# Attention and routed experts on one core: split parts stored once, tables stored in parts of five and three tiles, far rows on GpSimd's queue, shares spread by TensorE

## The chip, the core and the metric

The kernel runs on one core of a Trainium2 chip, in one launch. The metric is the device time of the program in microseconds (us), as a median over runs. The engines are TensorE (PE; its weight loads are PEld), VectorE (DVE), ScalarE (ACT), GpSimd (POOL) and SyncE (SP), which only issues transfers and waits. One core has 16 DMA engines.

## The reference, cut to what matters

`x` is 4 x 1024 tokens of 256 features, and every layernorm is over the features.

```python
h = layernorm(x)
q, k, v = h @ Wq + bq, h @ Wk + bk, h @ Wv + bv            # 16 heads of 16
pos_k = rel_embeddings @ Wk + bk                            # 128 relative positions
c2p = take_along_axis(q @ pos_k.T, clip(rel + 64, 0, 127))
p2c = swapaxes(take_along_axis(k @ pos_k.T, clip(-rel + 64, 0, 127)))
probs = softmax((q @ k.T + c2p + p2c) / sqrt(48))
out = (probs @ v) @ Wo + bo + h
x = x + layernorm(layernorm(out) * ln_scale + ln_bias)
y = layernorm(x)                                            # then 8 experts, top 1
e = argmax(softmax(y @ Wr + br))
# every expert sees y where it was chosen and zeros elsewhere; all eight results are added
x = x + layernorm(sum_i(relu((y * (e == i)) @ W1[i] + b1[i]) @ W2[i] + b2[i]))
```

`rel` is a log bucket of the distance: within 128 positions it varies, and beyond that it is constant on either side ("far").

## The kernel before, in words

The program has five stages, one after another, each a block that all engines enter and leave together.

`spread` (to 38 us) makes the position tables and stores them.

`project` (38 to 200 us) walks over 8 groups of 512 tokens. It normalises them, turns them with PE, makes q, k and v, and splits q and k into three bf16 parts (high, middle, low) so that bf16 products can stand for f32 ones. The parts are stored in `split_d` as six slots of each side, because an attention product uses six pairs of parts: one part goes to three slots, one to two, one to one. SP issues 12 stores of a group in L363. Small far products go to `far_d` (L369), normalised rows plus `bo` to `xn_d` (made by POOL in L551), and v to `v_d`.

`attend` (200 to 1490 us) walks over 64 units (4 batches x 16 heads), each of 8 tiles of 128 queries. Each unit first has its position products made by PE (`make_table`, two units ahead). ACT copies them out (L859), SP writes them to DRAM (`skew_write`, L655) and, when they have landed, reads them back skewed by one element for each row (`skew_read`, L665). POOL then mends the edges of the band in five steps (`edge`, L926 to L942). After the last step of a half it raises `near_made`, for which the PE products of that half of the tiles wait (`score`, L740). The order on SP for each pass `u` is written out by hand:

```python
skew_read(u + 1, 1); skew_write(u + 2, 0); load_unit(u + 4); store(u - 2)
skew_read(u + 2, 0); skew_write(u + 2, 1)
```

`load_unit` reads the six slots of q and of k of one unit, 96 rows of 2 KB on each side, in one transfer each (L637), and the far rows in three small ones (L642). It waits until the unit that used the buffers has been flipped: for unit u + 4 that is the last flip of unit u - 2, which PE makes in step 8u + 4, just ahead of the scores of tile 4 of unit u (`LAG` is 13 steps).

PE's order in step s is: flip half 0 of unit-tile s - 13, make table s + 16, flip half 1, score s, weigh s - 14, and in the second step of a unit `turn_top` (L785), which waits for five small POOL operations (`split_top`). POOL's order is also written out, by step s: the entries of `steps` say in which step which steps of `edge` of which half are made.

`mix` (1490 to 1690 us) walks over 16 groups of 256 tokens: heads and softmax shares are loaded, multiplied, projected by Wo, normalised three times and stored, with the routing behind it. In each of its first 8 steps 1 MB of W2 is loaded (L1119). `experts` (1690 to 2002 us) does the experts' products.

Of the kernel before, what the change touches and what calls it, by code (L numbers as in the profile page):

```python
# [35 lines left out]
QSLOTS = ((0, 1, 3), (3, 1, 2), (5, 1, 1))  # L36
KSLOTS = ((1, 2, 3), (2, 2, 2), (0, 1, 1))
# [16 lines left out]
def constants():  # L54
# [28 lines left out]
    steps[:, ET + 8 + P:] = np.arange(NT)[None, :] * P + np.arange(P)[:, None] + 1  # L83
    sel = np.zeros((P, E), np.float32)
    for j in range(4):
        sel[32 * j:32 * j + E] = 1.0 - np.eye(E)
    return dict(c_pick=pick, c_masks=masks, c_fold=fold, c_side=side, c_steps=steps, c_sel=sel)


def build(nc, x, Wq, bq, Wk, bk, Wv, bv, Wo, bo, rel_emb, ln_s, ln_b, W1, b1, W2, b2, Wr, br,  # L90
          c_pick, c_masks, c_fold, c_side, c_steps, c_sel, out):
    ctx = ExitStack()
    with ctx:
        sem = Rack(lambda name: ctx.enter_context(nc.semaphore(name)))

        def dram(name, shape, dt=F32):
# [3 lines left out]
        xn_d = dram("xn_d", [TOK, D])  # L100
        split_d = dram("split_d", [2, TERMS, N * DH, S], BF16)
        far_d = dram("far_d", [2, N, 2, PARTS, S], BF16)
# [8 lines left out]

        spread(nc, sem, Wk, bk, rel_emb, c_pick, c_masks, c_side, pick_d, posT_d)
        spent = sem.spend()
        project(nc, sem, spent, x, Wq, bq, Wk, bk, Wv, bv, bo, c_masks, posT_d, xn_d, split_d, far_d, v_d)
# [8 lines left out]
        mix(nc, sem, spent, x, xn_d, ctx_d, share_d, Wo, ln_s, ln_b, Wr, br, b1, W2, b2, c_masks, c_steps, c_sel, rows_d, bias_d,  # L123
            total_d, w2_all, idx_in, idx_out, expert)
# [44 lines left out]
def spread(nc, sem, Wk, bk, rel_emb, c_pick, c_masks, c_side, pick_d, posT_d):  # L169

    with ExitStack() as ctx:
# [26 lines left out]
        def _(sp):  # L198
# [9 lines left out]
            for tab in range(2):  # L208
                for n, (first, step, many) in enumerate((KSLOTS, QSLOTS)[tab]):
                    for slot in range(first, first + step * many, step):  # L210
# [57 lines left out]
def project(nc, sem, spent, x, Wq, bq, Wk, bk, Wv, bv, bo, c_masks, posT_d, xn_d, split_d, far_d, v_d):  # L268
# [5 lines left out]
    with ExitStack() as ctx:  # L274
# [8 lines left out]
        bv_b, bo_b = sb("bv_b", [P, D]), sb("bo_b", [P, D])  # L283
# [4 lines left out]
        xnb = [sb(f"xnb{i}", [P, GT, D]) for i in range(2)]  # L288
        v32 = [sb(f"v32_{i}", [P, GT, VROW]) for i in range(2)]
        stats, mv = sb("stats", [P, 2, GT, 6]), sb("mv", [P, 2, GT, 2])  # L290
        var, root, inv, shift = (sb(w, [P, 2, GT]) for w in ("var", "root", "inv", "shift"))
# [13 lines left out]
        xn_out, xnb_made = [sem(f"p_xn_out{i}") for i in range(2)], sem("p_xnb_made")  # L305
# [17 lines left out]
        def _(sp):  # L323
# [7 lines left out]
            for semaphore in spent:  # L331
# [7 lines left out]
                     (bv_b[:, :], view(bv.tensor, 0, [[0, P], [1, D]])),  # L339
                     (bo_b[:, :], view(bo.tensor, 0, [[0, P], [1, D]]))]  # L340
            assert len(loads) == 8
# [6 lines left out]
            for s in range(-2, NG + 1):  # L348
                g = s + 2
                if live(g):  # L350
                    sp.wait_ge(xnb_made, g + 1)
                    sp.dma_start(view(xn_d, g * G * D, [[D, P], [P * D, GT], [1, D]]), xnb[g % 2][:, :, :]
                                 ).then_inc(xn_out[g % 2], 16)
                    if live(g + XB):
                        load(g + XB)
                g = s - 1
                if live(g):
                    b, half = g // 2, g % 2
                    sp.wait_ge(lo_made, g + 1)
# [7 lines left out]
                    for m in range(4):  # L367
                        at = (m // 2 * N + b * H + m % 2 * 8) * 2 * PARTS * S + half * G
                        sp.dma_start(view(far_d, at, [[PARTS * S, 16], [S, PARTS], [1, G]]),  # L369
                                     far_part[g % 2][32 * m:32 * m + 16, :, :]).then_inc(far_out[g % 2], 16)  # L370
# [5 lines left out]
            for i in range(2):  # L376
                sp.wait_ge(v_out[i], 16 * (NG // 2))
                sp.wait_ge(split_out[i], 16 * 12 * (NG // 2))
                sp.wait_ge(far_out[i], 16 * 4 * (NG // 2))
                sp.wait_ge(xn_out[i], 16 * (NG // 2))  # L380

        @block.vector
        def _(dve):
# [3 lines left out]
            for s in range(-3, NG + 1):  # L387
                g = s + 2
                if live(g):
                    dve.wait_ge(root_made, g + 1)  # L390
                    nc.vector.reciprocal(inv[:, g % 2, :], root[:, g % 2, :]).then_inc(inv_made, 1)
                    dve.wait_ge(inv_made, g + 1)
                    nc.vector.scalar_tensor_tensor(shift[:, g % 2, :], mv[:, g % 2, :, 0], -1.0, inv[:, g % 2, :],
                                                   ALU.mult, ALU.mult).then_inc(shift_made, 1)
# [26 lines left out]
                if live(g):  # L421
                    if g == 0:
                        dve.wait_ge(loaded, 16 * 9)
# [15 lines left out]
        def _(act):  # L439
# [4 lines left out]
            def normal(g, t):  # L444
                if t == 0:
                    act.wait_ge(shift_made, g + 1)
                    if g >= NB:
                        act.wait_ge(x_turned, g - NB + 1)
                        act.wait_ge(xnb_made, g - NB + 1)
# [1190 lines left out]
```

## Time and profile before

| | |
|---|---|
| median of 3 runs | 2007.51 us (2007.21 to 2009.05) |
| profiled execution, its own time | 2003.63 us |
| span of the profile | 2001.7 us |
| busy in the span | PE 85%, DVE 68%, ACT 56%, POOL 53%, PEld 58% |
| moved by DMA | 453.36 MB, mean 226 GB/s |
| queue of SP | 415.25 MB, 65.2% of the 16 engines' time |
| SP's stores of parts | 32 of 384 KB, 32 of 256 KB, 32 of 128 KB |

A share of busy time is a mean over stages that have different limits. "DMA share" is the mean busy share of the 16 DMA engines: 0.5 can mean all of them half of the time, or eight of them all of the time. A wait of SP counts from its last instruction.

### The profile page before, as it was taken

How to read it: one execution, taken by the hardware profiler on the slowest of the kernel's cores; microseconds unless marked ns; L12 is line 12 of the kernel's file. 1: busy time of each engine (PE TensorE's matmuls, PEld its weight loads, DVE VectorE, ACT ScalarE, POOL GpSimd, SP SyncE). 2: the span in 40 equal slices, each digit the busy share in tenths (PEclk: the TensorE clock that was granted, in tenths of full speed). 3: DMA queues.
4: the chain of work that ended last, by engine and by line, in shares of the span. 5: the costliest groups of instructions: out<-in, count | busy, mean ns of one | idle time of the engine just before them, and what ended most of it. 6: DMA issues, size and time to landing. Idle time of an engine off the chain costs nothing. (4 is left out here: it accounts for less than half of the span.)

```text
span 2001.7 us, 40568 instructions
## 1 busy us (share of the span) xinstructions
PE 1698.0 (85%) x13688; PEld 1159.6 (58%) x13688; DVE 1370.7 (68%) x3938; ACT 1121.8 (56%) x2233; POOL 1069.1 (53%) x1268
## 2 busy tenths in 40 slices
PE   1882389999999999999999999999973674999997
PEld 1451156565656566566565666566532464999996
DVE  1673188788888788898798899899843553343343
ACT  1672257676767677677677777677751460222221
POOL 0210267676777667667576777777711451233332
PEclk6996589999999999999999999999996675999998
DMA  4598778777777777777877777787718852676772
GB/s 113 188 303 274 225 250 262 246 237 251 245 261 248 256 247 240 257 254 245 265 237 251 249 261 250 240 272 246 235 44 215 284 176 86 198 212 215 223 219 78
DMA packets 320826, 453.36 MB, mean 226 GB/s; under 512 B 35132, under 2 KB 260303, under 8 KB 320526
## 3 DMA queue, kind: packets, MB, share of 16 engines
q1 hardware_dynamic: 308034, 415.25, 65.2%
q10 hardware_dynamic: 7596, 21.10, 3.4%
q0 software_dynamic: 4992, 14.43, 1.9%
q8 instruction: 112, 1.84, 0.4%
q14 instruction: 92, 0.75, 0.1%
HBM read 257.32 MB, written 193.65 MB: 225 GB/s over the span
## 5 line engine op out<-in xcount | busy, mean ns | idle before, releaser
L865 ACT ACTIVATE t_probsT<-t_flip 128x512 f32<-128x512 f32 x1024 | 619.2, 607 | 242.7 <-PE t_flip L756 117.5
L814 DVE TENSOR_REDUCE t_most<-t_scores 128x1 f32<-128x640 f32 (+1 forms) x512 | 436.7, 853 | 169.8 <-PE t_scores L740 166.5
L833 DVE TENSOR_SCALAR t_band<-t_band,t_top 128x384 f32<-128x384 f32 (+1 forms) x512 | 383.8, 750 | 0.0
L859 ACT COPY t_table<-t_table_ps 128x512 f32<-128x512 f32 x512 | 298.2, 582 | 70.7 <-issue 41.1
L777 PE MATMUL t_sum_ps<-t_probsT,t_vals 128*32 128x256 f32 x4096 | 329.5, 394 | 0.2 <-ACT t_probsT L865 0.2
L926 POOL TENSOR_TENSOR t_near<-t_near,t_masks 128x384 f32<-128x384 f32 (+1 forms) x128 | 146.8, 1147 | 338.9 <-DMA t_near<-skew_d 336.4
L942 POOL TENSOR_TENSOR t_near<-t_near,t_masks 128x768 f32<-128x768 f32 (+1 forms) x128 | 272.4, 2129 | 0.0
L763 PE MATMUL t_flip<-t_masks,t_band 128*128 128x128 f32 x1408 | 263.0, 276 | 0.0
L818 DVE CUSTOM_DVE_ANT_0 t_band<-t_scores,t_near 128x384 f32<-128x384 f32 (+1 forms) x512 | 262.1, 512 | 0.0
L740 PE MATMUL t_scores<-t_masks,t_near 128*128 128x128 f32 x1408 | 243.5, 277 | 7.1 <-POOLq L945 7.1
L733 PE MATMUL t_scores<-t_after,t_quest 105*128 105x256 bf16 (+3 forms) x1024 | 244.9, 289 | 2.6 <-DVE t_most L818 2.4
L740 PEld LDWEIGHTS t_scores<-t_masks,t_near 128*128 128x128 f32 x1408 | 182.7, 143 | 46.6 <-POOLq L945 8.7
L712 PE MATMUL t_table_ps<-t_rows,t_quest 96*128 96x256 bf16 x512 | 143.5, 280 | 69.1 <-DMA t_before<-far_d 49.8
L733 PE MATMUL t_scores<-t_before,t_quest 105*128 105x256 bf16 (+3 forms) x768 | 195.0, 294 | 0.0
L763 PEld LDWEIGHTS t_flip<-t_masks,t_band 128*128 128x128 f32 x1408 | 164.7, 143 | 4.8
L756 PE MATMUL t_flip<-t_quest,t_before 108*128 108x512 bf16 (+3 forms) x512 | 161.4, 316 | 0.8 <-ACT t_probsT L865 0.7
L756 PE MATMUL t_flip<-t_quest,t_after 108*128 108x512 bf16 (+3 forms) x512 | 158.7, 310 | 1.2 <-DMA t_quest<-t_topT 0.8
L1606 PE MATMUL e_hid_ps<-e_xT,e_w 128*128 128x128 f32 x1248 | 148.0, 278 | 5.6 <-DMA e_total<-total_d 5.2
L1606 PEld LDWEIGHTS e_hid_ps<-e_xT,e_w 128*128 128x128 f32 x1248 | 147.5, 194 | 8.2 <-issue 5.5
L939 POOL TENSOR_TENSOR t_near<-t_near,t_masks 128x384 f32<-128x384 f32 (+1 forms) x128 | 145.5, 1137 | 0.0
L714 PE MATMUL t_table_ps<-t_rows,t_after 96*128 96x256 bf16 x512 | 142.9, 279 | 0.0
L1588 PE MATMUL e_out_ps<-w_all,e_hid 128*128 x624 | 141.0, 379 | 0.0
(186 smaller groups left out, 2343.7 us busy)
## 6 DMA issues: line engine op xcount, KB each, us to landing
skew_d<-t_table SPq DMA_DIRECT2D x128, 1024.0 KB, 8.9
t_near<-skew_d SPq DMA_DIRECT2D x128, 640.0 KB, 6.2
t_near<-skew_d SPq DMA_DIRECT2D x128, 384.0 KB, 4.8
e_w<-in_L_ffn_W_dram ACTq DMA_DIRECT2D x39, 512.0 KB
e_w<-in_L_ffn_W_dram SPq DMA_DIRECT2D x39, 512.0 KB
split_d<-p_part SPq DMA_DIRECT2D x32, 384.0 KB
t_after<-split_d SPq DMA_DIRECT2D x64, 192.0 KB
t_quest<-split_d SPq DMA_DIRECT2D x64, 192.0 KB
```

The costliest lines, as they stand in the source:

```text
L733: nc.tensor.matmul(out[:, at:at + size], quest[i][0:XROWS, t * P:(t + 1) * P], keys[0:XROWS, piece[0] * P:piece[0] * P + size], start=at % ...
L740: last = nc.tensor.matmul(out[:, (j - lo) * P:(j - lo + 1) * P], near[n % 2][:, 1, j, (t - j + 1) * P:(t - j + 2) * P], ident, start=False ...
L756: last = nc.tensor.matmul(out[:, (a - lo) * P:(z - lo) * P], keys[:, j * P:(j + 1) * P], quest[i][:, a * P:z * P], start=first, stop=False ...
L763: last = nc.tensor.matmul(out[:, (t - lo) * P:(t - lo + 1) * P], band[n % 2][:, t, at:at + P], ident, start=False, stop=True, is_transpose ...
L777: last = nc.tensor.matmul(sum_ps[32 * g:32 * g + 32, 0:2 * P], vals[b % 2][:, j, h * VDIM:h * VDIM + 32], probsT[s % 3][:, g * 2 * P:(g + ...
L814: nc.vector.tensor_reduce(most[:, c, 1:2], out[:, wide:S], AX.X, ALU.max)
L818: nc.vector.tensor_tensor_reduce(band[n % 2][:, t, 0:wide], out[:, 0:wide], near[n % 2][:, 0, t, at:at + wide], 1.0, -3.0e38, ALU.add, ALU ...
L833: nc.vector.tensor_scalar(band[n % 2][:, t, 0:wide], band[n % 2][:, t, 0:wide], top[n % 2][:, t:t + 1], None, ALU.subtract).then_inc(level ...
L859: nc.scalar.copy(table[n % 2][:, h, :, u % 4, :], table_ps[:, :, :]).then_inc(table_kept, 1)
L865: nc.scalar.activation(probsT[s % 3][:, half * 512:(half + 1) * 512], flip_ps[half][:, :], ACT.Exp, scale=SCALE).then_inc(expd, 1)
L942: nc.gpsimd.tensor_tensor(tail, tail, masks[:, 1, :].unsqueeze(1).unsqueeze(1).to_broadcast([P, 2, many, P]), ALU.mult).then_inc(edge_made, 1)
L1606: last = nc.tensor.matmul(hid_ps[s % 2][:, c, :], w1[s % WB][:, f, c * P:(c + 1) * P], xT[s % 2][:, f, :], start=(f == 0), stop=(f == 1))
```

## The change

It edits four stages.

In `project`, each of the three parts is stored once: a slot order is chosen in which q's parts are stored as (hi, mid), (mid, lo) and hi, so one store can take two neighbours; SP issues 6 stores of a group with half the bytes. `far_part` is stored whole, in one transfer of 384 KB where it was four of 48 KB. `xn_d`, its POOL operation and its stores are gone, and the reciprocals of the deviations stay in SBUF (`inv_all`).

In `attend`, the six slots are put together on reading. `load_unit` issues six transfers of 32 rows each, whose outermost dimension in DRAM is 2 (two parts, or one part named twice); before, it was two of 96 rows with an outermost dimension of 6. The far rows are loaded by POOL (`load_far`, three transfers) in its step t = 2, ahead of everything else of that step, behind the same wait for the flip. A table's halves are 5 and 3 tiles in the write and 4 and 4 in the read, where they were 4 and 4, and 3 and 5. PE waits for the second half at tile 4 instead of 3. All edge steps of the second half now come behind `split_top`, and its last one is in the step in which `load_far` comes first.

In `mix`, the shares are loaded once as 16 rows and spread to the heads' 128 partitions by PE (two products for each group, `spread_share`); `bo` is added by a product of one row. The residual is computed from `x` and `inv_all`. W2 is loaded in every second step.

```diff
-QSLOTS = ((0, 1, 3), (3, 1, 2), (5, 1, 1))
-KSLOTS = ((1, 2, 3), (2, 2, 2), (0, 1, 1))
+QSLOTS = ((0, 1, 5), (2, 3), (4,))
+KSLOTS = ((0, 2, 4), (1, 3), (5,))
...
-        split_d = dram("split_d", [2, TERMS, N * DH, S], BF16)
-        far_d = dram("far_d", [2, N, 2, PARTS, S], BF16)
+        split_d = dram("split_d", [2, PARTS, N * DH, S], BF16)
+        far_d = dram("far_d", [B, 4, 32, PARTS, S], BF16)
...
                     for m in range(4):
-                        for n, (first, step, many) in enumerate((QSLOTS, KSLOTS)[m // 2]):
-                            at = ((m // 2 * TERMS + first) * (N * DH) + b * D + m % 2 * P) * S + half * G
-                            sp.dma_start(view(split_d, at, [[S, P], [step * N * DH * S, many], [1, G]]),
-                                         part[g % 2][:, n, m, :].unsqueeze(1).to_broadcast([P, many, G])
-                                         ).then_inc(split_out[g % 2], 16)
+                        mine = at + m // 2 * (PARTS * part_at) + m % 2 * (P * S)
+                        takes = ((0, 2, 1), (2, 3, 0)) if m < 2 else ((0, 3, 0),)
+                        for a, z, slot in takes:
+                            sp.dma_start(view(split_d, mine + slot * part_at, [[S, P], [part_at, z - a], [1, G]]),
+                                         part[g % 2][:, a:z, m, :]).then_inc(split_out[g % 2], 16)
...
-            part, far = N * DH * S, PARTS * S
+            part = N * DH * S
+            pair, one, both = [[S, 2 * DH], [1, S]], [[S, DH], [1, S]], [[part, 2], [S, DH], [1, S]]
...
-                for dst, side_at in ((after[i], TERMS * part), (quest[i], 0)):
-                    sp.dma_start(dst[0:KROWS, :], view(split_d, side_at + n * (DH * S), [[part, TERMS], [S, DH], [1, S]])
-                                 ).then_inc(hats_in[i], 16)
+                at_q, at_k = n * (DH * S), PARTS * part + n * (DH * S)
+                for dst, src_at, dims in ((after[i][0:2 * DH, :], at_k, both), (after[i][2 * DH:4 * DH, :], at_k, both),
+                                          (after[i][4 * DH:KROWS, :], at_k, [[2 * part, 2]] + one),
+                                          (quest[i][0:2 * DH, :], at_q + part, [[0, 2]] + one),
+                                          (quest[i][2 * DH:4 * DH, :], at_q + 2 * part, [[0, 2]] + one),
+                                          (quest[i][4 * DH:KROWS, :], at_q, both)):
+                    sp.dma_start(dst, view(split_d, src_at, dims)).then_inc(hats_in[i], 16)
...
+            def load_far(n):
+                i, far = n % BUFS, PARTS * S
+                if n >= BUFS:
+                    pool.wait_ge(flipped, 2 * QT * (n - BUFS + 1))
+                far_q = ((n // H * 4 + n % H // 8) * 32 + n % 8 * 2) * far
+                far_k = far_q + 2 * 32 * far
+                for dst, far_at, many in ((quest[i][FAR:FAR + 6, :], far_q, 2 * PARTS),
+                                          (after[i][KROWS:FAR, :], far_k + far, PARTS),
+                                          (before[i][KROWS:FAR, :], far_k, PARTS)):
+                    nc.gpsimd.dma_start(dst, view(far_d, far_at, [[S, many], [1, S]])).then_inc(far_in[i], 16)
...
-            steps = ((2, 0, (0, 1)), (3, 0, (2,)), (4, 0, (3,)), (5, 0, (4,)),
-                     (6, 1, (0, 1)), (7, 1, (2,)), (8, 1, (3,)), (9, 1, (4,)))
+            steps = ((3, 0, (0, 1)), (4, 0, (2,)), (5, 0, (3,)), (6, 0, (4,)), (8, 1, (0, 1)), (9, 1, (2, 3)), (10, 1, (4,)))
...
             for s in range(-AHEAD, TS):
                 u, t = s // QT, s % QT
+                if t == 2 and 3 <= u + 4 < N:
+                    load_far(u + 4)
                 if t == 0 and 0 <= u + 1 < N:
                     keep_side(u + 1, 1)
-                if t == 4 and 0 <= u + 2 < N:
+                if t == 5 and 0 <= u + 2 < N:
                     keep_side(u + 2, 0)
...
-                if s < E:
-                    sp.dma_start(w2_all[:, s * KC:(s + 1) * KC, :], W2[s, :, :].rearrange("(c p) n -> p c n", p=P)
-                                 ).then_inc(w2_in[s // 4], 16)
+                if s % 2 == 1 and s // 2 < E:
+                    e = s // 2
+                    sp.dma_start(w2_all[:, e * KC:(e + 1) * KC, :], W2[e, :, :].rearrange("(c p) n -> p c n", p=P)
+                                 ).then_inc(w2_in[e // 4], 16)
...
+            def spread_share(g):
+                if g >= 2:
+                    pe.wait_ge(headsT_made, g - 1)
+                b, at = g // 4, g % 4 * (G * P)
+                for k in range(2):
+                    last = nc.tensor.matmul(share_ps[g % 2][:, k, :], which[:, k, :], share[:, b, at:at + G * P],
+                                            start=True, stop=True)
+                last.then_inc(share_made, 1)
```

## Rows read from the trace of the kernel before

**Rows 1.** Busy time by stretch (us; instructions), granted PE clock, DMA share, GB/s

```profile
core 0: us, PE busy (x) PEld busy (x) DVE busy (x) ACT busy (x) POOL busy (x), PEclk, DMA share, GB/s
100.00:150.00 50.00, 44.85 (x177) 25.29 (x179) 37.33 (x44) 35.35 (x48) 8.64 (x3) 1.00 0.92 303
...
700.00:900.00 200.00, 192.12 (x1774) 120.95 (x1773) 176.91 (x505) 147.87 (x284) 141.07 (x175) 0.99 0.76 248
...
1500.00:1600.00 100.00, 46.87 (x148) 35.32 (x148) 41.43 (x158) 30.64 (x70) 32.19 (x26) 0.65 0.87 247
```

**Rows 2.** SP's own waits, 300 to 1400 us (total, times, longest)

```profile
SPq L662 <- DMA skew_d<-t_table: 670.7, 111, 8.3
```

**Rows 3.** The writes of L655: duration ns min/median/max, first and last start

```profile
L655 SPq DMA_DIRECT2D skew_d<-t_table x128: 525/567/1772, 221.1 to 1439.8; - x128
```

**Rows 4.** SP's timeline over one pass of attention (start us, us)

```profile
583.36 0.93 SPq L665 DMA_DIRECT2D t_near<-skew_d  x2
584.39 0.56 SPq L655 DMA_DIRECT2D skew_d<-t_table  x1
585.00 0.75 SPq L637 DMA_DIRECT2D t_after<-split_d  x1
...
593.87 1.21 SPq L665 DMA_DIRECT2D t_near<-skew_d  x2
...
602.06 0.93 SPq L665 DMA_DIRECT2D t_near<-skew_d  x2
```

**Rows 5.** Busy time by stretch, columns as in Rows 1: short stretches

```profile
218.40:220.40 2.00, 1.20 (x4) 0.27 (x4) 0.00 (x0) 0.66 (x2) 0.00 (x0) 0.50 0.39 148
...
505.60:507.00 1.40, 1.40 (x16) 1.12 (x13) 1.36 (x6) 0.94 (x2) 1.40 (x3) 1.00 0.00 0
...
583.50:602.80 19.30, 19.16 (x185) 12.25 (x178) 18.98 (x52) 14.54 (x29) 14.57 (x20) 1.00 0.76 247
...
100.00:110.00 10.00, 8.41 (x40) 5.14 (x39) 7.06 (x6) 7.15 (x11) 2.42 (x1) 1.00 1.01 340
```

**Rows 6.** SP's timeline in the mix stage

```profile
1559.07 0.64 SPq L1119 DMA_DIRECT2D w_all<-in_L_ffn_W_dram  x1
...
1568.08 1.39 SPq L1119 DMA_DIRECT2D w_all<-in_L_ffn_W_dram  x1
...
1599.12 1.49 SPq L1084 DMA_DIRECT2D m_heads<-ctx_d  x2
...
1604.81 1.62 SPq L1084 DMA_DIRECT2D m_heads<-ctx_d  x2
...
1625.09 0.36 SPq L1130 DMA_DIRECT2D rows_d<-m_x  x1
...
1630.02 0.36 SPq L1130 DMA_DIRECT2D rows_d<-m_x  x1
```

**Rows 7.** The gathers of L1477, the only transfers that POOL issues without scattering

```profile
L1477 POOL DMA_INDIRECT e_rows<-rows_d,idx_in x39: 942/967/1167, 1688.5 to 1954.3; - x39
```

**Rows 8.** POOL's groups by form, 300 to 1400 us (busy, mean ns)

```profile
L942 POOL TENSOR_TENSOR t_near<-t_near,t_masks 128x768 f32<-128x768 f32 x57 | 105.7, 1854 | 0.0
```

**Rows 9.** PE's timeline around the scores of tile 4

```profile
593.40 0.22 PE L733 MATMUL t_scores<-t_after,t_quest 105*128 105x128 bf16 x1
...
593.84 0.38 PE L740 MATMUL t_scores<-t_masks,t_near 128*128 128x128 f32 x2
```

**Rows 10.** Waits of all engines, 300 to 1400 us (total, times, longest)

```profile
PE t_table_ps L785 <- POOL t_top_part L962: 43.8, 42, 4.4
```

**Rows 11.** The project stage's high parts and stores (first and last start)

```profile
L363 SPq DMA_DIRECT2D split_d<-p_part x96: 455/690/1317, 83.2 to 191.8; - x96
L501 ACT CAST p_part<-p_qk x8: 1897/1898/1905, 67.0 to 168.9; 128x2048 bf16<-128x2048 f32 x8
```

**Rows 12.** All engines' timeline in the project stage, two groups' first products

```profile
69.76 3.70 PE L524 MATMUL p_qk_ps<-p_xT,p_wq 128*128 128x512 f32 x8
...
82.15 3.70 PE L524 MATMUL p_qk_ps<-p_xT,p_wq 128*128 128x512 f32 x8
```

More of the change, by code:

```diff
@@ L83, in constants @@
     steps[:, ET + 8 + P:] = np.arange(NT)[None, :] * P + np.arange(P)[:, None] + 1
+    heads = np.zeros((H, 2, P), np.float32)
+    for h in range(H):
+        heads[h, h // 8, h % 8 * DH:h % 8 * DH + DH] = 1.0
     sel = np.zeros((P, E), np.float32)
@@ L208, in _ @@
             for tab in range(2):
-                for n, (first, step, many) in enumerate((KSLOTS, QSLOTS)[tab]):
-                    for slot in range(first, first + step * many, step):
+                for n, slots in enumerate((KSLOTS, QSLOTS)[tab]):
+                    for slot in slots:
                         for c in range(2):
@@ L347, in _ @@
                 load(g)
[L348 to L355, printed above, removed]
+            for s in range(NG + 1):
+                if live(s + XB):
+                    load(s + XB)
                 g = s - 1
@@ L586, in attend @@
         vals = [sb(f"vals{i}", [P, QT, VROW]) for i in range(2)]
-        table = [sb(f"table{i}", [P, 2, 2, 4, SPOT]) for i in range(2)]
+        table = [sb(f"table{i}", [P, 2, QT, SPOT]) for i in range(2)]
         side = [sb(f"side{i}", [P, 2, QT]) for i in range(2)]
@@ L970, in _ @@
             nc.gpsimd.memset(before_rows[0:3, :], 1.0).then_inc(before_set, 1)
+            for n in range(3):
+                load_far(n)
             pool.wait_ge(const_in, 16)
@@ L1005, in mix @@
         masks, steps = sb("masks", [P, 5, P]), sb("steps", [P, ET + 8 + P + NT])
-        heads, share = ([sb(f"{w}{i}", [P, 2, G * P]) for i in range(BUFS)] for w in ("heads", "share"))
+        heads = [sb(f"heads{i}", [P, 2, G * P]) for i in range(BUFS)]
+        share, which, bo_row = sb("share", [H, B, S]), sb("which", [H, 2, P]), sb("bo_row", [1, D])
         totals, inverse = sb("totals", [P, 4 * P]), sb("inverse", [P, 4 * P])
-        xn = [sb(f"xn{i}", [P, G, D]) for i in range(BUFS)]
         xt = [sb(f"xt{i}", [P, G, D]) for i in range(XBUFS)]
@@ L1107, in _ @@
                      (wr[:, :, :], Wr.rearrange("(k p) n -> p k n", p=P)),
-                     (br_b[:, :], row(br, E)), (steps[:, :], c_steps)]
-            assert len(loads) == 7
+                     (br_b[:, :], row(br, E)), (steps[:, :], c_steps),
+                     (which[:, :, :], c_heads), (bo_row[:, :], view(bo.tensor, 0, [[D, 1], [1, D]]))]
+            assert len(loads) == 9
             for dst, src in loads:
                 sp.dma_start(dst, src, allow_slow_non_contiguous=True).then_inc(loaded, 16)
-            for g in range(BUFS):
-                load(g)
+            load(0)
+            load(1)
+            sp.wait_ge(inverse_made, 1)
+            sp.dma_start(share_d[:, :].rearrange("n (a v) -> (n a) v", a=2), inverse[:, :]).then_inc(share_out, 16)
+            load(2)
+            sp.wait_ge(share_out, 16)
+            sp.dma_start(share[:, :, :], view(share_d, 0, [[S, H], [H * S, B], [1, S]])).then_inc(share_in, 16)
+            load(3)
             for dst, src in [(b1_sb[:, :, :], b1.rearrange("e (c p) -> p e c", p=P)), (b2_sb[:, :], b2),
```

166 lines of the change are left out of this document (77 added, 89 removed).

## The prediction

> **What bounds the kernel now.** I read the busy time by stretch first. In attention, 1290 of the 2002 us, PE is busy 96% of the time at a clock of 0.99 [rows 1], so PE looks like the bound. SP's own waits come next: SP waits 670.7 us of 1100 for its table writes to land [rows 2]. Its timeline shows why: in one pass it issues reads, a write and the loads, waits for the write, issues reads and a write, waits again [rows 4]. A pass takes (1439.8 - 221.1) / 63.5 = 19.2 us [rows 3], in the one shown 602.06 - 583.36 = 18.7. So two loops are almost equally tight, PE's work and SP's two round trips, and what lengthens either lengthens the stage. `project` is bound by DMA (share 0.92, 303 GB/s) and so is much of `mix` (0.87 at 247 GB/s, PE clock 0.65) [rows 1].
>
> **How many engines a transfer runs on.** This decides the case. In 218.4 to 220.4 us almost nothing but loads of L637 is under way: the share is 0.39, or 6.2 of 16 engines, with 148 GB/s [rows 5]. Full, the queue has a share of 1.01 and 340 GB/s [rows 5]. The loads' outermost dimension is 6. They all take the same six: in `mix`, heads and shares have an outermost dimension of 8. If these 512 KB of a step sit on the same eight engines (64 KB each) and the other 2 MB (x, normalised rows, stores, W2) on all sixteen (128 KB each), the loaded eight have 192 KB at 340/16 = 21.3 GB/s, 9.2 us; without W2 they have 128 KB, 6.2 us. The steps take 1568.08 - 1559.07 = 9.0 us and 1604.81 - 1599.12 = 5.7 us [rows 6]. Spread evenly they would be 7.7 and 4.6 us. So I take it that a transfer uses as many engines as its outermost dimension has entries, and always the same ones. The new loads have 2.
>
> The Trainium skill, "DMA: Bandwidth & Descriptors", section "Why a DMA increments its semaphore by 16 and not by 1", says that the engine count is the largest number up to 16 that divides both sides' slowest dimension, and that SP's queue takes the lowest-numbered engines. By that rule the loads go from six engines to engines 0 and 1; the trace agrees for six (0.39) and shows no transfer on two.
>
> **The change in attention.** One unit's loads are 2 x 192 KB. At 148 / 6.2 = 23.9 GB/s each [rows 5], they are 16.5 us of one engine: 2.7 us on each of six, 8.2 us on each of two. The whole pass occupies 0.76 x 16 x 19.3 = 235 us of engine time [rows 5]; without the loads that is 13.7 us on every engine. So the busiest engines have 16.4 us of 19.2 now and 21.9 us after. In addition the rings run empty between a landing and the next reads; such a stretch of 1.4 us with a share of 0.00 is in [rows 5]. Now there are two of them a pass (19.2 - 16.4 = 2.8). After, the loads fill the first and the second stays: 21.9 + 1.4 = 23.3 us, up to 24.7 if both stay. The bound from below takes the 4.13 MB of tables and results at 340 GB/s, 12.7 us: 12.7 + 8.2 + 1.4 = 22.3 us. The queue is in order, so reads issued behind the loads wait for them, and each wait in L662 for a write ends with its slowest engine; nothing covers the 8.2 us.
>
> The second cost is on POOL. In its step t = 2 of unit u, `load_far` waits for the flip that PE makes in step 8u + 4. Behind it in POOL's queue stands the last edge step of the second half, which raises `near_made`, and for that PE waits in the very same step 8u + 4. So after the flip follow three DMA issues and the last edge step, with PE idle. POOL's only issues here, gathers of 128 rows, take 0.97 us each [rows 7]; SP's far rows had six or three runs, and nothing shows such an issue on POOL, so I take 0.97 with 0.4 as the lower bound: 2.9 us (1.2). The edge step takes 1.85 us [rows 8]. PE covers the first 593.84 - 593.40 = 0.44 us with score products [rows 9]. Stall: 2.9 + 1.85 - 0.44 = 4.3 us (2.6). Against it stands a gain: PE's wait for `split_top`, 43.8 us of 57 units, 0.8 each [rows 10], should go, since the edges that wait for reads no longer stand ahead of it. PE's loop: 19.2 + 4.3 - 0.8 = 22.7 us (21.0 to 24.5, the latter if the idle PE loses a tenth of its clock).
>
> The two loops run side by side, so the pass takes the longer: 23.3 from the rings, 22.7 from PE. They don't fit exactly into each other; I take 23.7, which is 4.5 us more, for 60 of the 64 units (the loads stop four units early): +270 us. The 5 and 3 tiles move 0.25 MB of each pass between the round trips and change no sum. SP saves three issues and makes four more, inside its wait of L662: nothing. The first unit's loads take 8.2 instead of 2.7 us: +5.
>
> **The change in `project`.** SP's store bytes of a group fall from 3 to 1.5 MB, the 0.5 MB of `xn_d` go, far rows grow by 0.2 MB. Groups now follow each other every (168.9 - 67.0) / 7 = 14.6 us [rows 11]; PE's products alone repeat every 82.15 - 69.76 = 12.4 us [rows 12]. The rest of a group is 3 MB, 9 us at 340 GB/s, so PE and ACT set the pace: 12.4 to 13.6, minus 7 to 15 us over seven groups. The last high part is started at 168.9 and the last store issued at 191.8 [rows 11]; that is mostly backlog. Half the issues and bytes leave 10 to 14 of these 23 us: minus 9 to 13. Together -21 (-16 to -28).
>
> **The change in `mix`.** The eight busy engines get 32 KB of heads, 48 KB of x and stores and 32 KB of W2: 112 KB, 5.4 us, instead of 9.2, but 5.7 us [rows 6] before and the steps without loads (1630.02 - 1625.09 = 4.9 us [rows 6]) show that compute is near. PE gets four more products a step while its clock stands at 0.65 [rows 1], and the first step waits for the store and load of the shares with a PE product behind them. I take -8 us (0 to -20). Experts are unchanged.
>
> **Sum.** 2003.6 (the profiled execution's own time) + 270 + 5 - 21 - 8 = 2249.6, so 2250 us. It lies 4 us under the median of the runs, which is small beside the uncertainty.
>
> **The rivals.**
> - Only POOL's chain binds: the new loads are spread over six engines or more. For it: no transfer on two was seen. Against: sixes and eights both held. 2003.6 + (22.7 - 19.2) x 60 - 24 = 2190 us.
> - Only the rings bind, as POOL's issues are cheap and PE has slack: 23.3 a pass, 2003.6 + 246 - 24 = 2226 us. It differs from the forecast by little, and belongs to its range.
> - PE, often idle, drops to the lower clock for part of each pass, and reads land later on engines that run loads at the same time: 25 us a pass, 2003.6 + 348 - 24 = 2328 us. The clock column would show it.
> - Faster: the order of POOL's queue frees PE. The place is `split_top` in L785. If loads spread and the three issues end before PE's flip matters, a pass loses 0.8 us instead of gaining: 2003.6 - 48 - 29 = 1927 us. It decides only if the pass grows by less than 29 / 60 = 0.5 us, which a stall of even 1.3 us in the tile 4 step exceeds. The wait in the code is for an event of PE's own step, so only the size can be wrong.
>
> **How the numbers follow.** Both loops as described (with the rings alone): 0.65. POOL's chain alone: 0.16. The slower case: 0.12. Faster or unchanged: 0.07 (faster 0.05, within 0.2% 0.01, and 0.01 for slower by something small). 0.2% is about what a measurement of this kernel can tell from no change. Low end: PE's lower loop of 21.0, +108 - 24 = 2088, and the rings' lower bound of 22.3 us gives 2166; I set 2120. High end: 25 us a pass, 2328; I set 2330. Slower: 0.94.
>
> **What would show it.** Right: in a pass of about 23.5 us the DMA share is near 0.62 with long stretches of 0.12 (two engines); SP's waits in L662 grow to over 900 us in total; L740 gains PE idle time of 2 to 4 us a unit behind POOL's L942; L785's wait is gone; DMA_DIRECT2D on POOL takes 0.4 to 1 us; project's high parts start every 13 us; mix steps take 5 to 7 us. Wrong: loads alone at a share of 0.39 or more, POOL's issues under 0.4 us, or an attention stage of some 1290 us.

## The result

The changed kernel takes 2299.7 us (median of 4 runs, 2289.76 to 2300.41); the kernel before takes 2007.36 (4 runs). The ratio is 1.1451, with a 95% interval of 1.1412 to 1.1489: slower, inside the predicted range (2120 to 2330), and 50 us above the predicted 2250. The profiled execution took 2300.41 us, its span is 2298.6 us. Of all the executions told of below, one, of 2918 us at a granted clock of 0.55 (in the run with the old order of edges), is left out of its ratio.

Where the time went is read first from the stages. A stage starts with the first transfer that SP issues for it (`p_xt` for project, `t_rows` for attention, `m_totals` for mix, `e_w` for the experts):

| us | project | attention | mix | experts |
|---|---|---|---|---|
| before | 161.8 | 1292.9 | 196.3 | 312.6 |
| after | 133.4 | 1577.8 | 236.1 | 312.9 |
| measured change | -28 | +285 | +40 | 0 |
| predicted change | -21 | +275 | -8 | 0 |

Busy time by stretch of the changed kernel, in attention and in mix (columns as in [rows 1]):

```profile
700.00:900.00 200.00, 171.77 (x1439) 104.69 (x1437) 141.89 (x409) 119.77 (x230) 126.14 (x170) 0.89 0.63 206
1840.00:1860.00 20.00, 20.00 (x56) 13.68 (x54) 9.19 (x42) 8.17 (x20) 8.03 (x8) 0.50 0.54 160
```

In attention everything is less busy than in [rows 1], the rings too (0.63 for 0.76), and PE's clock fell from 0.99 to 0.89: a loop of waits sets the pace. In mix it is the opposite: PE works for all of the 20 us, at the lower clock of 1.2 GHz.

The waits of all engines in the changed kernel, 300 to 1600 us (total, times, longest), and in the second fence SP's own:

```profile
POOL t_quest L908 <- PE t_flip L752: 236.1, 55, 4.4
...
PE t_scores L729 <- POOLq L946: 184.7, 54, 5.9
```

```profile
SPq L650 <- DMA skew_d<-t_table: 358.8, 59, 8.6
SPq L643 <- ACT t_table L848: 258.4, 101, 5.4
SPq L659 <- ACT t_made L874: 173.2, 52, 6.4
```

PE waits once a unit, 184.7 / 54 = 3.4 us, for the `near_made` that POOL raises after its last edge step; POOL has waited 4.3 us for PE's flip just before. SP no longer waits for its writes alone, as in [rows 2]: 432 us go to waits for ACT, so SP has slack. PE's wait for `split_top` [rows 10] is in no row of this view any more. POOL's timeline shows the chain (start us, us):

```profile
709.71 0.56 POOL L908 DMA_DIRECT2D t_quest<-far_d  x1 [4.38 <-PE t_flip L752]
710.26 0.53 POOL L908 DMA_DIRECT2D t_after<-far_d  x1
710.78 0.52 POOL L908 DMA_DIRECT2D t_before<-far_d  x1
711.31 1.81 POOL L943 TENSOR_TENSOR t_near<-t_near,t_masks 128x768 f32<-128x768 f32 x1
```

Three issues, 1.61 us, then the edge step, 1.81 us: the 3.4 us. How long a pass is can be read from the writes, as in [rows 3]:

```profile
L643 SPq DMA_DIRECT2D skew_d<-t_table x128: 518/552/3342, 197.6 to 1694.4; - x128
```

(1694.4 - 197.6) / 63.5 = 23.6 us, where it was 19.2.

### The profile page after: what moved, and what is told of

Same layout as the page of the kernel before. It is cut to its first block and busy times, and to the rows that moved or that the text cites. A ratio compares the mean times of both kernels' runs of the same rounds, so it can differ in the third digit from the quotient of the medians.

```text
span 2298.6 us, 40964 instructions
## 1 busy us (share of the span) xinstructions
PE 1894.7 (82%) x13816; PEld 1248.9 (54%) x13816; DVE 1355.4 (59%) x3954; ACT 1127.7 (49%) x2233; POOL 1140.8 (50%) x1452
## 5 line engine op out<-in xcount | busy, mean ns | idle before, releaser
L729 PE MATMUL t_scores<-t_masks,t_near 128*128 128x128 f32 x1408 | 279.9, 309 | 218.5 <-POOLq L946 218.5
L822 DVE TENSOR_SCALAR t_band<-t_band,t_top 128x384 f32<-128x384 f32 (+1 forms) x512 | 365.0, 713 | 0.0
L766 PE MATMUL t_sum_ps<-t_probsT,t_vals 128*32 128x256 f32 x4096 | 361.3, 428 | 0.2 <-ACT t_probsT L854 0.2
L729 PEld LDWEIGHTS t_scores<-t_masks,t_near 128*128 128x128 f32 x1408 | 205.6, 160 | 281.0 <-POOLq L946 237.2
L752 PE MATMUL t_flip<-t_masks,t_band 128*128 128x128 f32 x1408 | 272.3, 284 | 0.0
L722 PE MATMUL t_scores<-t_after,t_quest 105*128 105x256 bf16 (+3 forms) x1024 | 270.6, 311 | 0.7 <-DVE t_most L807 0.6
L943 POOL TENSOR_TENSOR t_near<-t_near,t_masks 128x1024 f32<-128x1024 f32 (+1 forms) x128 | 267.4, 2089 | 0.7
L745 PE MATMUL t_flip<-t_quest,t_after 108*128 108x512 bf16 (+3 forms) x512 | 178.1, 348 | 0.5 <-ACT t_probsT L854 0.3
L927 POOL TENSOR_TENSOR t_near<-t_near,t_masks 128x512 f32<-128x512 f32 (+1 forms) x128 | 145.7, 1138 | 39.2 <-DMA t_near<-skew_d 28.1
L908 POOL DMA_DIRECT2D t_quest<-far_d x64 | 35.6, 557 | 251.6 <-PE t_flip L752 251.6
L940 POOL TENSOR_TENSOR t_near<-t_near,t_masks 128x512 f32<-128x512 f32 (+1 forms) x128 | 145.1, 1134 | 0.0
```

The source lines that it names most:

```text
L722: nc.tensor.matmul(out[:, at:at + size], quest[i][0:XROWS, t * P:(t + 1) * P], keys[0:XROWS, piece[0] * P:piece[0] * P + size], start=at % ...
L729: last = nc.tensor.matmul(out[:, (j - lo) * P:(j - lo + 1) * P], near[n % 2][:, 1, j, (t - j + 1) * P:(t - j + 2) * P], ident, start=False ...
L745: last = nc.tensor.matmul(out[:, (a - lo) * P:(z - lo) * P], keys[:, j * P:(j + 1) * P], quest[i][:, a * P:z * P], start=first, stop=False ...
L752: last = nc.tensor.matmul(out[:, (t - lo) * P:(t - lo + 1) * P], band[n % 2][:, t, at:at + P], ident, start=False, stop=True, is_transpose ...
L766: last = nc.tensor.matmul(sum_ps[32 * g:32 * g + 32, 0:2 * P], vals[b % 2][:, j, h * VDIM:h * VDIM + 32], probsT[s % 3][:, g * 2 * P:(g + ...
L822: nc.vector.tensor_scalar(band[n % 2][:, t, 0:wide], band[n % 2][:, t, 0:wide], top[n % 2][:, t:t + 1], None, ALU.subtract).then_inc(level ...
```

## The experiments

Each run is told with its attention and mix stages, read as above. All ratios are to the kernel before, on the same chip. Three groups: which loop binds attention, what else in attention costs, and what mix costs.

### Far rows issued behind the edges of step 6

```diff
-                if t == 2 and 3 <= u + 4 < N:
-                    load_far(u + 4)
...
                         for step in of:
                             edge(n, h, step)
+                if t == 6 and 3 <= u + 4 < N:
+                    load_far(u + 4)
```

> The changed kernel, with POOL's loads of the far rows moved from the head of step t = 2 behind the last edge step of t = 6, where the flip they wait for has long been made. Its attention stage takes 1578 us, some 24.0 us a pass. If POOL's queue sets that pass (the flip, three issues of 1.61 us together, the last edge step of 1.81 us, and PE idle for 3.4 us and at a lower clock after it), the pass falls to what is next, the two loaded DMA engines: one pass of the changed kernel shows 754.24 - 732.30 = 21.9 us between the reads, waits for tables included, so 21 to 22 us, 2300 - (2 to 3) x 58 = 2125 to 2185 us, and the clock in attention rises from 0.88. If the engines with the loads already set the pass (23.3 us as forecast), it stays at 23.3 or more: 2260 to 2300 us, with PE waiting as long as now but for reads.

2222.77 us, ratio 1.1084 (1.1045 to 1.1124). Attention 1502 us: 76 less than after, 209 more than before. That is between the two ranges, so neither theory alone holds: the chain on POOL costs something beside the rings, but most of the time stays when it is gone. What POOL waits for now is the table reads, 6.4 us each time (its waits, 300 to 1600 us); in the changed kernel POOL has no such wait:

```profile
POOL t_near L927 <- DMA t_near<-skew_d: 369.8, 58, 10.1
```

### Loads of 16 rows each

```diff
-                for dst, src_at, dims in ((after[i][0:2 * DH, :], at_k, both), (after[i][2 * DH:4 * DH, :], at_k, both),
-                                          (after[i][4 * DH:KROWS, :], at_k, [[2 * part, 2]] + one),
-                                          (quest[i][0:2 * DH, :], at_q + part, [[0, 2]] + one),
-                                          (quest[i][2 * DH:4 * DH, :], at_q + 2 * part, [[0, 2]] + one),
-                                          (quest[i][4 * DH:KROWS, :], at_q, both)):
-                    sp.dma_start(dst, view(split_d, src_at, dims)).then_inc(hats_in[i], 16)
+                for dst, at, parts in ((after[i], at_k, (0, 1, 0, 1, 0, 2)), (quest[i], at_q, (1, 1, 2, 2, 0, 1))):
+                    for slot, p in enumerate(parts):
+                        sp.dma_start(dst[slot * DH:slot * DH + DH, :], view(split_d, at + p * part, one)
+                                     ).then_inc(hats_in[i], 16)
```

> The changed kernel, with the six loads of 32 rows of a unit (outermost dimension 2) replaced by twelve of 16 rows (outermost dimension 16), so that each is spread over sixteen DMA engines; the same bytes, six more issues on SP. If POOL's queue sets the pass, nothing but a few tenths of a us changes: 2270 to 2300 us, and SP only waits longer for tables. If the two loaded engines set it, they lose 7 of their 22 us and the pass falls to the 22.7 us or less of POOL's loop: under 2240 us.

2275.74 us, ratio 1.137 (1.1337 to 1.1403). Attention 1560 us: only 18 less than after. Its waits, 300 to 1600 us, have the same row as after:

```profile
PE t_scores L727 <- POOLq L944: 184.7, 54, 5.9
```

With the rings relieved, PE waits for POOL exactly as long as before. So in the changed kernel it is POOL's chain that sets the pass, not the rings.

### Both together

The two edits above in one kernel.

> Both edits: loads over sixteen engines and far rows loaded late. Either theory expects the attention stage back at that of the kernel before, 1293 us, or up to 45 us less as PE's wait for the split of the maxima is gone: 2300 - 285 - (0 to 45) = 1970 to 2015 us. The project stage keeps its gain of 28 us and the mix stage its loss of 40 us. If it stays above 2050 us, a third cost in attention is still there (the 5 and 3 tiles, or the other order of the edges).

2063.39 us, ratio 1.0315 (1.0279 to 1.0351). Attention 1340 us. Together the edits give back 238 us, alone 76 and 18. That is the signature of two loops side by side: each alone holds most of the time, and relieving one shows the other. But 47 us above before stay, which neither explains: the third cost that the expectation named.

### The kernel before, with its loads in pairs

```diff
-                    sp.dma_start(dst[0:KROWS, :], view(split_d, side_at + n * (DH * S), [[part, TERMS], [S, DH], [1, S]])
-                                 ).then_inc(hats_in[i], 16)
+                    for j in range(3):
+                        sp.dma_start(dst[2 * j * DH:2 * (j + 1) * DH, :],
+                                     view(split_d, side_at + n * (DH * S) + 2 * j * part, [[part, 2], [S, DH], [1, S]])
+                                     ).then_inc(hats_in[i], 16)
```

> The kernel before, with nothing changed but the loads of the parts: three transfers of two slots for each side (outermost dimension 2) in place of one of six. The rings alone, without POOL's loads. If all six go to the same two engines, these have 21.9 us of work in a pass and the ring stands empty for at least 1.4 us: 21.9 to 23.3 us a pass against 19.2, 2007 + (2.7 to 4.1) x 60 = 2170 to 2255 us, and a DMA share near 0.12 while they alone are under way. If the engines are not the bound, SP's three round trips hide them: 2000 to 2030 us.

2242.24 us, ratio 1.1185 (1.1161 to 1.121). Attention 1536.5 us: (1536.5 - 1292.9) / 60 = 4.1 us more for each pass with loads, which is 23.3 us. Same bytes, same order, far rows on SP: an outermost dimension of 2 where it was 6, and 237 us. Its 700 to 900 us:

```profile
700.00:900.00 200.00, 172.63 (x1478) 106.76 (x1477) 139.75 (x416) 123.02 (x236) 115.14 (x143) 0.91 0.64 210
```

A share of 0.64 is far from full, and yet the rings are the bound: two of them are. The engine count can be read directly where loads alone are under way, at the start of the stage and inside a pass (columns as in [rows 1]):

```profile
218.00:223.00 5.00, 2.41 (x8) 0.53 (x8) 0.23 (x1) 1.88 (x4) 0.00 (x0) 0.50 0.14 50
723.00:728.00 5.00, 5.00 (x53) 3.16 (x47) 4.16 (x14) 4.24 (x8) 1.31 (x2) 1.00 0.14 49
```

A share of 0.14 is 2.2 of 16 engines, at 50 GB/s, where the loads of before had 6.2 engines and 148 GB/s [rows 5]. For some 5 us of a pass hardly anything but two engines works. The rings hold PE by way of POOL: PE's wait for `split_top`, 43.8 us in [rows 10], is 182.2 us here (300 to 1600 us). In the changed kernel such stretches are there too, but shorter (751 to 753 us: 0.13 to 0.14).

### Attention of before, loads of 16 rows

The changed kernel's `attend` replaced by that of before, with its `load_unit` reading each part in transfers of 16 rows and the far rows from the new `far_d`, all on SP.

> The changed kernel with the attention stage of before the change (halves of 4 and 4 tiles stored, 3 and 5 read, far rows on SP, POOL's old order of edges and top), but each part still stored once and loaded as twelve transfers of 16 rows. It tells where the last 47 us of the attention stage come from, which it keeps when loads are spread and far rows are late (1340 us against 1293). Theory order (the halves, the order of POOL and its issues cost them): attention takes 1285 to 1295 us, the whole 2300 - 287 = 2013 us (2003 to 2020). Rival, loads (twelve transfers a unit and parts read two or three times cost them): attention takes 1330 us or more, the whole 2050 us or more.

1977.89 us, ratio 0.9874 (0.9817 to 0.9931): 1.3% less than before, although mix is still the long one (240 us). Attention 1254.7 us, 38 less than before and 85 less than with both cures, and below what either theory gave. So the cure of the loads goes beyond the damage: the six engines of before had been a cost too. 700 to 900 us:

```profile
700.00:900.00 200.00, 196.64 (x1837) 124.60 (x1837) 183.35 (x519) 152.39 (x295) 150.97 (x187) 1.00 0.79 258
```

PE is busy 98%: now PE is the bound. And the 85 us must lie in POOL's issues, in its order, or in the halves. Two runs take these apart.

### Both cures, far rows on SP; then the old order of edges as well

```diff
-            def load_far(n):
...
-                    nc.gpsimd.dma_start(dst, view(far_d, far_at, [[S, many], [1, S]])).then_inc(far_in[i], 16)
+                    sp.dma_start(dst, view(far_d, far_at, [[S, many], [1, S]])).then_inc(hats_in[i], 16)
```

The second of the two has this edit too:

```diff
-            steps = ((3, 0, (0, 1)), (4, 0, (2,)), (5, 0, (3,)), (6, 0, (4,)), (8, 1, (0, 1)), (9, 1, (2, 3)), (10, 1, (4,)))
+            steps = ((2, 0, (0, 1)), (3, 0, (2,)), (4, 0, (3,)), (5, 0, (4,)),
+                     (6, 1, (0, 1)), (7, 1, (2,)), (8, 1, (3,)), (9, 1, (4,)))
```

> The changed kernel with loads of 16 rows in twelve transfers and the far rows back on SP's queue, behind them; halves and POOL's order stay as changed. Against the run that had both cures (far rows late on POOL: attention 1340 us) only POOL's issues are gone. Between that and the old order (1255 us) lie 85 us. Theory issues (1.6 us a pass on POOL ahead of or between edges, and their queue): attention 1255 to 1285 us, the whole 1965 to 2000 us. Theory order (all edges of the second half behind the five small operations of the top, so that near_made comes late): attention 1315 us or more, the whole 2030 us or more. Between these: both.

> The run before it in this list, and POOL's steps of edges as before the change (2 to 5 and 6 to 9 instead of 3 to 6 and 8 to 10). What is left of the change in attention is then the cut of the halves (5 and 3 tiles written, 4 and 4 read). Theory order: attention falls to 1255 to 1270 us, the whole to 1965 to 1985 us. Theory halves (4 tiles edged and read last instead of 3, and the wait at tile 4): attention stays above 1290 us. If the run before it is already at 1270 us or less, this one tells only whether the order matters at all: 1250 to 1275 us.

2112.91 us (1.0547, 1.0494 to 1.0601) and 2121.94 us (1.0586, 1.0564 to 1.0607). Attention 1388 and 1394 us. In the first, theory issues failed; the time lies in the open range of theory order, but above the 1340 us of the run with both cures, which no theory had foreseen. The second refutes theory order and is as theory halves had it. Far rows on SP are not better than on POOL but 48 us worse, and the order of the edges matters little (6 us, the wrong way). What the last run and the attention of before with loads of 16 rows still differ in is the cut of the halves, with its waits, and with it POOL's copy `keep_side`, made a step later (t = 5 for 4) and behind all ten edge steps of the table two units before instead of five: 1394 against 1255 us. This package costs 139 us here, and the prediction had said that the halves "change no sum". Which part of it costs was not run.

SP's timeline of one pass with the new halves (this last run), then with the old ones (the run before these two):

```profile
713.68 0.91 SPq L657 DMA_DIRECT2D t_near<-skew_d  x2
714.70 0.53 SPq L647 DMA_DIRECT2D skew_d<-t_table  x1
715.27 5.34 SPq L625 DMA_DIRECT2D t_after<-split_d  x6
720.96 3.54 SPq L625 DMA_DIRECT2D t_quest<-split_d  x6
...
726.12 0.99 SPq L657 DMA_DIRECT2D t_near<-skew_d  x2
727.22 0.53 SPq L647 DMA_DIRECT2D skew_d<-t_table  x1
734.57 0.92 SPq L657 DMA_DIRECT2D t_near<-skew_d  x2
```

```profile
710.81 0.93 SPq L653 DMA_DIRECT2D t_near<-skew_d  x2
711.84 0.53 SPq L643 DMA_DIRECT2D skew_d<-t_table  x1
712.41 3.82 SPq L623 DMA_DIRECT2D t_after<-split_d  x6
716.27 2.85 SPq L623 DMA_DIRECT2D t_quest<-split_d  x6
...
720.82 1.48 SPq L653 DMA_DIRECT2D t_near<-skew_d  x2
722.40 0.53 SPq L643 DMA_DIRECT2D skew_d<-t_table  x1
728.91 0.93 SPq L653 DMA_DIRECT2D t_near<-skew_d  x2
```

The pass shown is 734.57 - 713.68 = 20.9 us in one and 728.91 - 710.81 = 18.1 in the other (over the stage, 139 / 64 = 2.2 us apart). Of these 2.8 us, 2.4 lie in the first round trip (12.4 to 10.0, from reads to reads; issuing twelve loads takes 9.2 us of SP for 6.7, in the passes just before and behind 8.1 to 8.4 for 6.5 to 7.0) and 0.4 in the second (8.45 to 8.1). In the two passes shown SP stands idle for only 0.1 and 0.3 us between its last issue and the reads, so the first trip ends with the issues, not with a landing. That also fits the 48 us for far rows on SP: three more issues, 720.16 - 719.16 = 1.0 us a pass with the old halves, stand on that path. Why the issues are slower behind a write of 5 tiles is not shown.

What stays open: whether the new halves cost anything without twelve loads behind the longer write. The kernel before with the halves alone was not run.

### Mix without the product that adds bo

The three runs that follow are read by their mix stage. Beside that, one number gives the spread: with the mix code of the changed kernel unaltered, the stage took from 225.2 us (both cures) to 240.0 us (attention of before, loads of 16 rows). This run leaves bo out of the result.

```diff
                     for k in range(2):
-                        nc.tensor.matmul(out_ps[g % 2][:, t, :], headsT[g % 2][:, k, t * P:(t + 1) * P],
-                                         wo[:, k, :], start=(k == 0), stop=False)
-                    last = nc.tensor.matmul(out_ps[g % 2][:, t, :], masks[0:1, 3, :], bo_row[:, :], start=False, stop=True)
+                        last = nc.tensor.matmul(out_ps[g % 2][:, t, :], headsT[g % 2][:, k, t * P:(t + 1) * P],
+                                                wo[:, k, :], start=(k == 0), stop=(k == 1))
```

> The changed kernel without the product that adds bo (bo is left out of the result); everything else stays. In the changed kernel mix takes 236 us where it took 196 before, its PE is busy 20.00 of 20 us at a clock of 0.50, and the bo products are 36.9 us of that (64 of them, two a step). Theory PE (mix is bound by PE's own products at the lower clock): the 2.3 us a step go, mix becomes 199 to 207 us, the whole 2300 - 33 = 2267 us (2258 to 2275); lower still if the clock then rises. Rival, shares (mix is long because the shares arrive late and each step waits for the chain between DVE and PE): mix stays at 230 us or more, the whole at 2292 us or more.

2232.62 us, ratio 1.1134 (1.1087 to 1.1181). Mix 171 us: 65 less, though the products that are gone were 36.9 us. The rest goes with the clock, in this stretch 0.89 and in the next 0.71:

```profile
1800.00:1820.00 20.00, 18.43 (x88) 13.82 (x87) 16.87 (x75) 15.27 (x35) 14.23 (x12) 0.89 0.88 277
```

### Mix with the shares loaded by DMA

`spread_share` is gone and the shares are loaded as in the kernel before, spread over the heads' partitions by the transfer; bo is still added by PE.

> The changed kernel with the shares loaded as before the change (spread by 512 KB of transfers for each pair of steps on the eight engines that also load the heads), bo still added by PE. It takes 29.6 us of PE products (64 of them) out of mix and the wait of the first products for the 16 rows of shares. Theory PE: mix becomes 205 to 212 us, the whole 2300 - 28 = 2272 us (2262 to 2280), with PE's clock still near 0.50 as its one-row products stay. Rival, DMA: the eight engines are the bound again in the steps with W2 (9.2 us), so the time stays within 8 us of the changed kernel's: 2292 us or more. Should the clock rise above 0.6 here but not without bo, the products of 16 rows are what keeps it low.

2272.35 us, ratio 1.1343 (1.1303 to 1.1382). Mix 209 us, 27 less than after (16 to 31 less by the spread above), about the 29.6 us of the products. The clock stays at 0.50 with PE never idle:

```profile
1840.00:1860.00 20.00, 20.00 (x57) 13.19 (x56) 9.36 (x37) 8.04 (x18) 7.43 (x6) 0.50 0.71 226
```

### The product that adds bo, over 128 rows

```diff
-                    last = nc.tensor.matmul(out_ps[g % 2][:, t, :], masks[0:1, 3, :], bo_row[:, :], start=False, stop=True)
+                    last = nc.tensor.matmul(out_ps[g % 2][:, t, :], masks[:, 4, :], bo_row[:, :], start=False, stop=True)
```

`masks[:, 4, :]` is the identity, and `bo_row` holds bo in every one of its 128 rows.

> The changed kernel; the 64 products that add bo stay as many and as wide (128 x 256 out), but contract over all 128 rows (the identity by a tile that holds bo in every row) instead of one row. In mix PE's granted clock was 0.50 throughout with the one-row products in (with and without the 16-row products of the shares), and 0.71 to 0.93 in the loaded steps without them, when mix took 171 us instead of 236. Theory clock (the one-row products are what holds the clock down): at the same count of products the clock rises above 0.65, and mix takes 171 us plus 64 x 0.45 = 29 us at most, so 175 to 205 us; the whole 2250 us (2235 to 2272). Rival, load (the clock is down because PE is never idle, whatever the rows): the clock stays at 0.50 and mix at 232 us or more, the whole at 2294 us or more.

2235.81 us, ratio 1.1152 (1.1131 to 1.1174). Mix 171 us, as without any bo product. Nothing but the rows of 64 products (the length of their contraction, with the load of bo that this needs) has changed, and the clock is at full (2.4 GHz):

```profile
1840.00:1860.00 20.00, 19.84 (x159) 15.22 (x157) 14.02 (x55) 12.91 (x31) 12.50 (x11) 1.00 0.71 236
```

The groups of PE in mix, first of the changed kernel (1750 to 1983 us), then of this one (1746 to 1930 us):

```profile
L1337 PE MATMUL m_out_ps<-m_wo,m_headsT 128*128 128x256 f32 x128 | 62.5, 640 | 4.2 <-DVE m_headsT L1162 4.2
L1339 PE MATMUL m_out_ps<-m_bo_row,m_masks 1*128 1x256 f32 x64 | 36.9, 674 | 0.0
L1347 PE MATMUL m_share_ps<-m_share,m_which 16*128 16x256 f32 x64 | 29.6, 615 | 25.8 <-DMA m_share<-share_d 25.8
```

```profile
L1337 PE MATMUL m_out_ps<-m_wo,m_headsT 128*128 128x256 f32 x128 | 36.2, 407 | 5.7 <-DVE m_headsT L1162 5.7
L1339 PE MATMUL m_out_ps<-m_bo_row,m_masks 128*128 128x256 f32 x64 | 19.6, 389 | 0.0
L1347 PE MATMUL m_share_ps<-m_share,m_which 16*128 16x256 f32 x64 | 19.5, 431 | 24.7 <-DMA m_share<-share_d 24.7
```

A product of one row took 674 ns and the same product over 128 rows 389. The products beside them, unchanged, went from 640 to 407 and from 615 to 431: it is the clock of the whole engine. So the time of mix hangs on the rows of these 64 products. But they do not hold the clock down at all times: the run with loads of 16 rows alone, with the same mix code as the changed kernel, had five us in the loaded half at full clock, four one-row products among them:

```profile
1820.00:1825.00 5.00, 5.00 (x28) 3.49 (x27) 3.77 (x11) 3.06 (x8) 2.85 (x3) 1.00 0.52 156
```

The stage took 226 us there, 10 less than after. What lets the clock rise for a while is not shown.

### Two versions meant to be fast

Both take the changed `project` and the attention of the 1977.89 us run. The first loads the shares by DMA and lets DVE make x times inverse plus bo (two more instructions a step); the second keeps PE's shares and lets POOL make it.

> The changed kernel's project stage, the attention of the run before it in this call (old order, loads of 16 rows), and a mix stage with shares loaded by DMA, x times inverse plus bo made by DVE in two more instructions a step, and W2 in every second step. If theory order and theory PE both hold: 2007 before, minus 28 for project, 0 to -8 for attention, and for mix 0 to -10 (256 KB less a step to load, PE as before): 1969 us (1958 to 1982). If twelve loads a unit cost 40 us: 2010 us. If DVE's 0.95 us more a step bind mix: 1985 us.

> Project as changed, attention of before with loads of 16 rows in twelve transfers, and mix as changed except that bo is added by POOL (x times inverse, plus bo, two operations of 128x512, 2.5 us a step) and no longer by PE. The best run so far (1927.8 us) has DVE busy 98% of the time in mix and takes 183 us there; without bo, with DVE as here and PE at a higher clock, mix took 171. If POOL, 3.8 us of some 7.5 us a step before, has room for 2.5 more: mix 171 to 180 us, the whole 1978 - 240 + 175 = 1913 us (1908 to 1924). If POOL becomes the bound (6.3 us a step and its waits): mix 185 to 200 us, the whole 1925 to 1940 us.

1927.76 us (0.9619, 0.9585 to 0.9652) and 1957.49 us (0.977, 0.9752 to 0.9788). The first is the fastest kernel run, faster than any of its three forecasts: attention 1259 us, mix 183. In mix DVE is now the bound:

```profile
1480.00:1500.00 20.00, 12.09 (x41) 8.93 (x42) 19.69 (x56) 10.60 (x24) 13.46 (x10) 0.73 0.75 243
```

The second was a miss: mix takes 215 us, more than either theory gave, with POOL busy 13.20 of 20 us and PE again near full at the lower clock:

```profile
1520.00:1540.00 20.00, 18.92 (x54) 14.16 (x54) 10.85 (x50) 10.39 (x23) 13.20 (x12) 0.50 0.52 160
```

It has no one-row products, so these alone don't decide the clock; what does in this run stays open. By the stages, bo over 128 rows in the 1977.89 us kernel would give 1977.89 - 240 + 171 = 1909 us; that sum was not run.

## Why the prediction was right, point by point

The forecast of 2250 us is 50 under the result: attention came out 10 us longer than forecast, project 7 shorter, mix 48 longer. That attention fits to 10 us is in part luck: the other of the two loops set the pace.

- **As many engines as the outermost dimension has entries.** Right, and in size: the rings alone were to take 23.3 us a pass, and in the kernel before with its loads in pairs they took 19.2 + 243.6 / 60 = 23.3. The share with loads alone was 0.14 there, for "stretches of 0.12". The rule of the Trainium skill, "DMA: Bandwidth & Descriptors", section "Why a DMA increments its semaphore by 16 and not by 1", is borne out for 2 as it was for 6. Which of the engines they are, no view here shows.
- **POOL's chain.** Right in its place: tile 4 of each unit, three issues and an edge step. The stall was taken as 4.3 us and is 3.4, since an issue takes 0.53 us, not the 0.97 of the gathers [rows 7]; with the measured terms its own sum gives 1.61 + 1.81 - 0.44 = 3.0, so the 0.44 us of cover did not show. The wait for `split_top` [rows 10] went, as said.
- **Which loop is longer.** This step failed. The prediction had the rings at 23.3 and PE's loop at 22.7 (21.0 to 24.5), and took 23.7 for both. The runs showed PE's loop to be the longer one. By itself, with the loads on sixteen engines, it took 19.2 + (1560.1 - 1292.9) / 60 = 23.7; the rings' loop by itself, with the far rows late, 19.2 + (1502.2 - 1292.9) / 60 = 22.7. Both together took 19.2 + (285 - 5) / 60 = 23.9. PE's stall is shorter than forecast, but PE is busy for 0.859 x 23.9 = 20.5 us where it was 0.961 x 19.2 = 18.4, at a clock of 0.89. That is near its upper bound, "if the idle PE loses a tenth of its clock". So +285 us where +275 stood, and SP's waits for its writes fell to 358.8 us instead of rising above 900.
- **The halves change no sum.** Wrong in the one setting where it was tried: 139 us with twelve loads a unit, `keep_side`'s later place included. In the changed kernel itself the term is not separated; with the same halves and twelve loads the stage was bound by POOL's chain (1560 us).
- **Project.** -21 predicted, -28 measured. The high parts follow each other every (152.65 - 66.64) / 7 = 12.3 us, at the lower end of the step's 12.4 to 13.6, which is 16 us over seven groups; from the last high part to attention it is 19 us where it was 31.
- **Mix.** This step failed in sign: -8 predicted, +40 measured. It said that PE "gets four more products a step while its clock stands at 0.65" and that compute is near, and then gave DMA the word. The runs showed PE to be the bound, in steps of (1901.84 - 1849.51) / 5 = 10.5 us (between the issues of `m_xt`), as the one-row products went with a clock of 0.50 for everything that PE did. Four more products need not cost anything. With 128 rows in their place the stage takes 171 us, 25 less than before, which is more than the gain that was predicted, and as much as with no bo product at all.

## What to carry to other kernels

When two loops are equally tight, undo them together before judging either: alone they gave back 76 and 18 us, together 238. Count the engines that a transfer runs on before its bytes, since fewer bytes in DRAM were bought here with a third of the engines; and once it runs on all sixteen, count SP's time to issue it. A small product on PE can cost more than its own time: the 36.9 us of one-row products went with 65 us of the stage, and the same number of products over 128 rows cost nothing (mix 171.1 us, 171.0 without any).

## What was not expected of the hardware

- 64 products of one row in the stage went with a granted clock of 0.50 in the loaded stretches of the changed kernel (1780 to 1900 us), the same 64 over 128 rows with 1.00. The products of 16 rows stayed in both. In another run of the same mix code the clock was at 1.00 for a few us all the same.
- A plain transfer of three to six rows of 2 KB costs POOL 0.52 to 0.56 us to issue.
- Twelve transfers of 32 KB took SP 6.5 to 7.0 us to issue in three passes with a write of 4 tiles ahead of them, and 8.1 to 9.2 us in three with one of 5.
- With transfers of two entries a mean DMA share of 0.64 was a full bound; alone, they ran at a share of 0.14 and 50 GB/s.
